# Decoder layers on one core: score and value products issued for two units at a time, then both kinds of transposes, then the 512-column products

## What is computed

```python
def local_attention(q, k, v):            # window 32: token i sees j with i - 32 <= j <= i
    sim = jnp.einsum('bhwie,bhwje->bhwij', bq, bk2) * QK_SCALE
    sim = jnp.where(mask, -jnp.finfo(sim.dtype).max, sim)
    attn = jax.nn.softmax(sim, -1)
    out = jnp.einsum('bhwij,bhwje->bhwie', attn, bv2)

def attn_layer(x, Wqkv, qs, ksc, Wo):
    q, k, v = jnp.split(x @ Wqkv, 3, -1)
    q = l2norm(q) * qs;  k = l2norm(k) * ksc
    q = q * cos * scale + rotate_half(q) * sin * scale
    k = k * cos / scale + rotate_half(k) * sin / scale
    return local_attention(q, k, v) @ Wo

def ffn_layer(x, g, bln, W1, b1, W2, b2):
    a, gate = jnp.split((layernorm(x) * g + bln) @ W1 + b1, 2, -1)
    return a * jax.nn.gelu(gate, approximate=False) @ W2 + b2
```

## Time and profile before

| | |
|---|---|
| median of 3 executions | 4276.14 us (4275.76 to 4276.42) |
| the profiled execution: its own time | 4277.26 us |
| its span, first to last instruction | 4275.5 us |
| busy over the span | PE 93%, DVE 82%, ACT 78%, POOL 72% |
| mean granted TensorE clock | 0.983 |

### The profile page before, as it was taken

One profiled execution on the slowest core, in us unless ns is written; L12 is line 12 of the kernel. 1 busy time (PEld: TensorE's weight loads), 2 busy tenths in 40 slices (PEclk: granted clock), 3 DMA queues, 4 the chain that ended last, 5 costly groups with the idle time before them and its releaser, 6 DMA issues.

```text
span 4275.5 us, 102722 instructions
## 1 busy us (share of the span) xinstructions
PE 3981.7 (93%) x30384; PEld 3060.7 (72%) x30384; DVE 3521.6 (82%) x11903; ACT 3326.0 (78%) x11558; POOL 3080.2 (72%) x3387
## 2 busy tenths in 40 slices
PE   7888887899999999999999999999999999999997
PEld 5777776677777777777777777777777777777774
DVE  5676665788888888888888888888888888888884
ACT  1455554788888888888888888888888888888885
POOL 2333332788888888888888888888888888888883
PEclk9999998899999999999999999999999999999997
DMA  4222221000000000000000000000000000000000
GB/s 147 80 80 80 80 82 61 22 5 2 2 2 7 22 2 2 2 1 27 2 2 2 2 7 22 2 2 2 7 22 2 2 2 2 8 2 2 2 2 20
DMA packets 76222, 86.74 MB, mean 20 GB/s; under 512 B 13622, under 2 KB 69396, under 8 KB 74836
## 3 DMA queue, kind: packets, MB, share of 16 engines
q1 hardware_dynamic: 75732, 80.87, 5.9%
HBM read 45.33 MB, written 35.52 MB: 19 GB/s over the span
## 4 chain that ended last, share of the span: by engine, by line
PE 75%; ACT 13%; issue 4%; DVE 4%; POOL 3%; DMA 0%; SPq 0%; DVEq 0%; POOLq 0%; ACTq 0%; PEldq 0%
PE bank_pair L1081 10%; PE bank L1092 9%; PE bank L1099 9%; PE bank L1146 8%; PE bank L453 7%; PE bank L1112 6%; PE bank L454 6%; PE bank L455 6%; ACT p L1258 3%; PE bank L1138 3%; PE bank_pair L557 1%; ACT L1207 1%; POOL xn_lo L1411 1%; PE bank L551 1%; PE bank L533 1%
## 5 line engine op out<-in xcount | busy, mean ns | idle before, releaser
L1258 ACT ACTIVATE p<-p,mx 128x128 f32<-128x128 f32 x3072 | 1194.8, 396 | 26.0 <-DVE mx L1341 25.4
L1416 POOL TENSOR_TENSOR rot<-own_crossed 128x512 f32<-128x512 f32 x768 | 986.2, 1284 | 296.8 <-DVE ri L1329 275.2
L1420 POOL TENSOR_TENSOR p<-p,ri 128x512 f32<-128x512 f32 x768 | 801.7, 1044 | 96.9 <-DVE ri L1329 96.8
L1341 DVE CUSTOM_DVE_ANT_0 p<-bank_pair,band_f 128x128 f32<-128x128 f32 x3072 | 701.8, 284 | 143.4 <-issue 136.5
L1405 POOL TENSOR_TENSOR rot<-rot,rn 128x512 f32<-128x512 f32 x768 | 806.3, 1050 | 11.4 <-ACT rn L1229 11.4
L1081 PEld LDWEIGHTS bank_pair<-qkT 64*128 64x128 f32 x6144 | 402.3, 186 | 306.1 <-issue 290.7
L1258 ACT ACTIVATION_READ_ACCUMULATOR p<-p,mx 128x1 f32 x3072 | 596.9, 194 | 0.0
L1350 DVE TENSOR_REDUCE ss<-sq 128x8 f32<-128x512 f32 x768 | 523.7, 682 | 72.5 <-ACT sq L1290 64.6
L453 PE MATMUL bank<-wqkv_hi,xs_lo 128*128 128x512 f32 x1152 | 526.9, 457 | 48.3 <-ACT rstd L1244 37.1
L1234 ACT ACTIVATE oT<-bank 128x256 f32<-128x256 f32 x768 | 291.8, 380 | 345.3 <-PE bank L1092 340.9
L1355 DVE COPY pTl<-bank 128x512 f32<-128x512 f32 x768 | 525.1, 684 | 36.9 <-PE bank L1112 32.4
(11 more groups left out here) (198 smaller groups left out, 7421.8 us busy)
## 6 DMA issues: line engine op xcount, KB each, us to landing
pos_scratch<-pos_sb SPq DMA_DIRECT2D x32, 1020.0 KB, 4.4
sc<-pos_scratch SPq DMA_DIRECT2D x32, 512.0 KB, 4.0
wqkv_raw<-in_L_ffn_Wqkv SPq DMA_DIRECT2D x6, 1536.0 KB, 6.6
ctx_sb<-in_ctx SPq DMA_DIRECT2D x32, 128.0 KB, 3.5
wo<-in_L_ffn_Wo SPq DMA_DIRECT2D x6, 512.0 KB, 3.8
mrow<-in_mask_BxS_fk SPq DMA_DIRECT2D x1, 2048.0 KB, 7.8
x_all<-in_x SPq DMA_DIRECT2D x4, 512.0 KB, 8.8
out<-res SPq DMA_DIRECT2D x8, 256.0 KB, 2.3
```

The source lines that it names most:

```text
L1258: last = nc.scalar.activation(p[:, j, h, :], p[:, j, h, :], ACT.Exp, bias=mx[:, j, h:h + 1], scale=-1.0, accum_out=psums[:, j, h:h + 1])
L1416: nc.gpsimd.tensor_tensor(rot[:, (k - 6) % 4, :, :], own[:, (k - 6) % 4, :, :], crossed[:, (k - 6) % 4, :, :], ALU.add).then_inc(L["rot0"], 1)
L1420: nc.gpsimd.tensor_tensor(p[:, j, :, :], p[:, j, :, :], ri[:, j, :].unsqueeze(2).to_broadcast([128, G, T]), ALU.mult).then_inc(L["pn"], 1)
```

## The change

PE's slots now differ. In odd slots S is issued for two units together (16 instructions), then PV for two units together (16 instructions), then T2, T1, and the 512-column products. In even slots there are only T2, T1, and the q and k products. To hold two units, S fills both halves of its two banks and PV fills all of bank 3; the WO result lies over the first part of the PV result in that bank, and the copy of PV by ACT (`oT`) is one instruction of 512 columns for two units. Buffers grow (`qkT` 2 to 4, `v_sb` 8 to 16, `p` with its sums 4 to 5, `pTl` 2 to 4). Stages move: v products from distance 9 to 7, T1 from 9 to 8, T2 from 13 to 15, PV from 15 to 18. The feed-forward steps move to other slots, and the order of the stages inside a slot changes on all four engines.

```diff
+        oT_ps, y_ps = banks[3][:, :], banks[3][:, 0:T]
+        s_ps = bank_pair[:, :, :]
...
-                if on(10):
-                    j = (k - 10) % 2
+                if on(10) and (k - 10) % 2 == 1:
                     pe.wait_ge(L["qkT"], n(10) + 1)
-                    if at.again(10, 1):
-                        pe.wait_ge(L["mx"], n(10))
+                    if at.again(10, 2):
+                        pe.wait_ge(L["mx"], n(10) - 1)
+                    for w in range(2):
+                        j = (k - 10 - 1 + w) % 4
+                        for h in range(G):
+                            r = slice(h % 2 * DL, h % 2 * DL + DL)
+                            c = 2 * w + h // 2
+                            last = nc.tensor.matmul(s_ps[:, h % 2, c * T:(c + 1) * T], qkT[r, j, h // 2, :], qkT[r, j, 2 + h // 2, :], start=True, stop=True)
+                    last.then_inc(L["S"], 1)
+                if at.ffn(9):
+                    pe.wait_ge(Fm["gate"], 3 * at.F + 2)
+                    gate(2)
+                if at.ffn(10):
+                    if at.values_at(9):
+                        pe.wait_ge(L["v"], at.P + 2)
...
+                    value(0)
+                if at.ffn(15):
...
+                    for c, (c0, m) in enumerate(FF_CHUNKS):
+                        last = nc.tensor.matmul(ffn_ps[:, :], w2[0:m, c, :], uf[0:m, c, :], start=(c == 0), stop=(c == 2))
+                    last.then_inc(Fm["y_mm"], 1)
+                if on(18) and (k - 18) % 2 == 1:
+                    pe.wait_ge(L["pT"], n(18) + 1)
+                    pe.wait_ge(L["v"], at.pair(18) + 1)
+                    if at.again(18, 2):
+                        pe.wait_ge(L["oT"], at.pair(18))
...
+                            last = nc.tensor.matmul(oT_ps[rows, c * T:(c + 1) * T], v_sb[:, u % 16, h, :], pTl[:, u % 4, h, :], start=True, stop=True)
+                    last.then_inc(L["PV"], 1)
+                if on(15):
+                    pe.wait_ge(L["pn"], n(15) + 1)
+                    if at.again(15, 1):
+                        pe.wait_ge(L["pT"], n(15))
...
                 if at.ffn(8):
                     if at.values_at(7):
+                        pe.wait_ge(L["v"], at.P + 1)
+                    else:
+                        pe.wait_ge(Fm["gate"], 3 * at.F + 1)
+                    gate(1)
+                if on(8):
+                    pe.wait_ge(L["rot"], n(8) + 1)
+                    if at.again(8, 1):
+                        pe.wait_ge(L["qkT"], n(8))
```

More of the change, by code:

```diff
@@ L878, in build @@
         rot = sb("rot", [128, 4, 2 * G, DL])
[L879 to L885, removed]
+        qkT = sb("qkT", [128, 4, 4, T])
+        v_sb = sb("v_sb", [128, 16, G, DL])
+        mx = sb("mx", [128, 5, G])
+        p = sb("p", [128, 5, G, T])
+        psums = sb("psums", [128, 5, G])
+        ri = sb("ri", [128, 5, G])
+        pTl = sb("pTl", [128, 4, G, T])
         oT = sb("oT", [128, 8, 2 * T])
@@ L1083, in emit @@
[L1083 to L1093, removed]
@@ L1104, in emit @@
                     else:
[L1105 to L1113, removed]
+                        pe.wait_ge(Fm["rstd"], at.F + 1)
@@ L1114, in emit @@
+                    pe.wait_ge(Fm["w1_split"], at.lf + 1)
+                    pe.wait_ge(Fm["xn"], at.F + 1)
+                    gate(0)
+                if at.ffn(13):
+                    if at.values_at(11):
+                        pe.wait_ge(L["v"], at.P + 3)
+                    else:
+                        pe.wait_ge(Fm["u"], 3 * at.F + 2)
+                    value(2)
                 if on(4):
@@ L1274, in emit @@
                     nc.scalar.activation(gain[:, :], vec_raw[:, 0:2], ACT.Copy).then_inc(Fm["gain"], 1)
-                if on(9) and k % 2 == 1:
-                    act.wait_ge(L["proj"], at.pair(9) + 1)
-                    if at.again(9, 8):
-                        act.wait_ge(L["PV"], n(9) - 6)
-                    nc.scalar.activation(v_sb[:, (k - 9) % 8:(k - 9) % 8 + 2, :, :].rearrange("p u h n -> p (u h n)"), v_ps[:, :], ACT.Copy).then_inc(L["v"], 1)
-                if at.renew() and k in (5, 7):
-                    round_group(UB + (k - 5) // 2)
+                if at.ffn(10):
+                    gelu(2)
+                    use_table(LOG_EXP_SET)
+                if on(12):
+                    j = n(12) % 5
+                    act.wait_ge(L["mx"], n(12) + 1)
+                    for h in range(G):
+                        last = nc.scalar.activation(p[:, j, h, :], p[:, j, h, :], ACT.Exp, bias=mx[:, j, h:h + 1], scale=-1.0, accum_out=psums[:, j, h:h + 1])
+                    last.then_inc(L["exp"], 1)
                 if at.ffn(9):
@@ L1285, in emit @@
                     gelu(0)
+                if on(8):
+                    act.wait_ge(L["T1"], n(8) + 1)
+                    if at.again(8, 4):
+                        act.wait_ge(L["S"], at.pair(8) - 1)
+                    nc.scalar.activation(qkT[:, (k - 8) % 4, :, :].rearrange("p c n -> p (c n)"), qkT_ps[:, :], ACT.Copy).then_inc(L["qkT"], 1)
                 if on(4):
@@ L1295, in emit @@
                     round_group(k)
-                if at.ffn(9):
-                    gelu(1)
+                if at.ffn(2):
+                    act.wait_ge(Fm["centre"], at.F + 1)
+                    act.wait_ge(Fm["gain"], at.lf + 1)
+                    nc.scalar.activation(xsq[:, :], ffn_ps[:, :], ACT.Square).then_inc(Fm["xsq"], 1)
+                    nc.scalar.activation(xcg[:, :], ffn_ps[:, :], ACT.Copy, scale=gain[:, 0:1]).then_inc(Fm["xcg"], 1)
+                if on(7) and k % 2 == 1:
+                    act.wait_ge(L["proj"], at.pair(7) + 1)
+                    if at.again(7, 16):
+                        act.wait_ge(L["PV"], at.pair(7) - 7)
+                    nc.scalar.activation(v_sb[:, (k - 7) % 16:(k - 7) % 16 + 2, :, :].rearrange("p u h n -> p (u h n)"), v_ps[:, :], ACT.Copy).then_inc(L["v"], 1)
+                if at.renew() and k in (3, 5):
+                    round_group(UB + (k - 3) // 2)
             use_table(LOG_EXP_SET)
```

280 lines of the change are left out of this document (118 added, 162 removed).

## The result

The changed kernel takes 4162.98 us (median of 4 executions, 4161.27 to 4167.14), the kernel before 4275.95 us (4 executions on the same chip). The ratio is 0.9737 [0.972, 0.9754]: 113 us less, where the prediction took off 161. The profiled execution has a span of 4160.3 us and a granted clock of 0.982.

What follows compares the result with a forecast made beforehand. PE was taken to fill the 71.65 us body. From 4277: -180 pairs, +14 size changes, -48 x 2.3 waits going, +48 x 2.3 coming, +5 ends = 4116, 4115 on the median's scale; range 4040 to 4205.

Steps and rivals of the forecast that it cites:

- Pairs, -0.47 us each: PE's S, PV and T1: two units pay the three size changes once instead of twice, 180 us less in all.
- a charge per unit: Rival: PE's charge belongs to each unit, not the size change, so pairing saves nothing: 4280 us; chance 0.03.
- the clock: Rival: eight transposes in a row on PE risk the lower clock level, then probably slower; chance 0.02.
- New size changes, 0.15 each: Slots 9 and 15: full-size work between S and PV adds changes, 0.3 us a body, 14 us in all.
- Waits that go: PE's waits for `oT`, `rstd` and `xn_lo` all disappear: 2.3 us a body less.
- Waits that come: New PE waits at slot 10 (1.3), slot 8 (0.7) and slot 7 (0.3): 2.3 us a body, bounds nothing to about 5.
- the seven steps listed for ACT: From PV's end in slot 9: `oT`, exponentials, table, GELU, `qkT`, squares, v copy; summed as 4.9 us.
- Ends, 5 us: Paid once, as units stay three slots longer in the pipeline: two or three thin slots of some 2 us.
- Another engine holds PE: Rival: PE catches up with DVE in plain pairs and waits, one to 2.5 us a body: 4165 to 4235; chance 0.16.
- Its own mark: Sign that another engine holds PE: PE waits on `mx` before S; no size given.
- Slower by bank 2: Rival: ACT lags and each of eight v copies is waited for 0.9 us, 7.2 a body: 4350 us; chance 0.05.
- The new waits don't come: Rival: slots even out and ACT may be early; half the 2.3 us missing gives 4060, all 4005; chance 0.14.

Runs made afterwards that it cites:

- Run 1: The changed kernel with PE in odd slots issuing S, PV, S, PV instead of both S and then both PV: 4361.49 us, ratio 1.0201.
- run 4: The changed kernel with the third gate (slot 9) and last feed-forward product (slot 15) ahead of S instead of between S and PV: 4226.86 us.
- Run 5: The changed kernel with POOL doing `xg` and `xn_lo` after the `rot` product of the same slot instead of first: 4142.39 us, ratio 0.9687.
- run 6: The changed kernel with the first value product of slot 10 behind T2 and T1 on PE instead of before them: 4161.69 us.
- run 10: The changed kernel with `rot` before `xg`, `xn_lo` on POOL, tables computed early, slot 10's first value product behind T2, T1 and `pTl` copied earlier there: 4137.04 us.
- run 7: The changed kernel with ACT in slot 9 copying v before the GELU table load and first GELU instead of after: 4218.34 us, ratio 0.9868.
- run 8: The changed kernel with ACT's v copy ahead of the GELU table and PE's first value product behind T2 and T1: 4217.14 us, ratio 0.9865.
- run 12: Changed kernel with POOL's `rot` before `xg`, `xn_lo` and early rotary tables (4140.73 us); in slot 9 ACT's four exponentials precede the `oT` copy: 4106.43 us.

## Why the prediction was right, and where its sum was off

- **Pairs, -0.47 us each.** Right to the second digit: 2.12 against 2.46 us for S and PV, and 0.13 around them. Run 1 gives 0.35 of it back. The two rivals that went against it (a charge per unit; the clock) are out: inside the doubled S group the spacing of 0.21 stands once, and the granted clock is 1.00 in every plain body, with transposes in runs of eight. Inside the stream it is 0.50 only in short stretches at the layer starts, and the kernel before has these at three of its five.
- **New size changes, 0.15 each.** As forecast. The largest doubt was full size to PV; last gate product to PV is 0.32 us, as into S. But in run 4, without them, the body is longer, so they aren't worth avoiding in that way.
- **Waits that go.** All three went. They were mis-sized: between starts, PE stood 2.9 us a body at such places before, not the 2.3 of the waits view, because the view counts from a matmul's recorded end. (In the distances of starts: 1.59 before 512-column products, 1.10 before WO, 0.20 between S and PV.)
- **Waits that come**, forecast 2.3, are the term that failed: 3.4 us a body between starts. Slot 10 has 1.6 (1.3), slot 7 0.4 (0.3), slot 8 0.5 (0.7). The 1.3 is a slip of addition: the seven steps listed for ACT (0.5, 1.56, 1.30, 0.54 and three times 0.5) make 5.4 us, not 4.9, and so a wait of 1.8. With it the term would have been 2.8 us a body and the forecast 24 us higher, 4139. Not in the list at all was T1 waiting for `rot`, 0.9, most of it in slot 7. The `rot` wait could have been read from POOL's new order: `xg` and `xn_lo` stand ahead of it. Run 5 shows that it costs 21 us, 0.35 us a body and the rest at the layer starts.
- So a plain body is 71.65 - 3.76 + 0.3 - 2.9 + 3.4 = 68.7, measured 68.75. The 0.55 over the forecast make 48 x 0.55 = 26 us. They are small by luck: the waits that came were 1.1 us a body longer than forecast, the ones that went 0.6.
- **Ends, 5 us**, left out the layer starts. These cost 5 x 4.2 = 21 us more. With the 26 that is 47 of the 48 us between 4115 and 4163.
- **The rivals.** "Another engine holds PE" is the nearest: no single engine is the bound, but at 89% busy DVE, 87% ACT and 86% POOL the waits move instead of going. That fits runs 1, 4, 6 and 10. Its own mark, PE waiting for `mx` before S, is 1.2 us in 32 bodies; that form of it is out. "Slower by bank 2" did not come. Its condition, ACT late at all eight hand-overs, is met at two. "The new waits don't come" is out as well: more came than were listed.

Left open: why PE's wait for `pTl` before T2 of an even slot, 0.1 us a body between starts in the changed kernel, grows to some 0.4 to 0.6 by the waits view in runs 1, 4, 6, 7 and 8 and in none of the others, and what the 6 us that run 12 still loses at a layer start (73.2 + 68.0 - 2 x 67.7 in the centre products) consist of. Run 12 with the value product of run 6 was not tried.

## What to carry to other kernels

On a TensorE that works with parts of its array, sort the work by size inside a slot: two units' 64-row products together, then two units' 64-column ones, took 0.47 us of size changes off a pair. The gain can be read before the change from distances of starts, as can the waits (the waits view showed 2.3 us of 2.9). When a rearrangement leaves several engines near 90%, read for each what idles just ahead of its unbroken run: moving PE's own wait (runs 6, 8, 10, each against the kernel without it) gained 1 to 4 us, no more than the spread of the executions, while filling ACT's gap of 2 us with work that was ready gained 34. List in the forecast what stands ahead of each producer on its own engine, for every slot, and for the places that come once a layer too; and add such a list up twice: half a microsecond dropped in a body that runs 48 times is 24 us.

## What the hardware showed that wasn't expected

A DVE multiplication of 128x128 elements, with both inputs in SBUF, took 0.28 us alone and up to 5.6 us beside POOL. It stood through as many as four boundaries between POOL instructions that followed each other without a gap (at 2403.62, 2404.62, 2405.85 and 2407.09 us of the changed kernel), and ended 0.15 us behind the last one:

```profile
2402.72 5.56 DVE L1346 TENSOR_TENSOR rot_tab<-rot_base,qk_scl 128x128 f32<-128x128 f32 x1
2407.09 1.04 POOL L1418 TENSOR_TENSOR rot<-rot,rn 128x512 f32<-128x512 f32 x1
```

In the kernel before it got in at a boundary: `rot_tab` took 0.8 to 1.4 us and ended 0.15 us behind a POOL addition that another POOL instruction followed at once; and the table's second multiplication there, 1.52 us instead of 0.68, lay beside a POOL instruction of 1.49 us instead of 1.05. The Trainium skill (SBUF — State Buffer, SBUF: two separate sides) says that a DVE operation with two SBUF inputs and a GpSimd operation that reads SBUF lock the shared ports for a whole instruction, whichever starts first, so that the other is blocked. The trace agrees that DVE is held while POOL works, and shows that the end of one instruction need not let the other in. What decides it stays open. DVE's other work, with an input in PSUM, ran beside POOL at its usual length (the `own_crossed` multiplications, 0.65 to 0.69 us in all 1536 of the changed kernel).
